# Attention in units of two key tiles by half of the queries, with projections for two heads at once through DRAM

## The reference

```python
lat = layer_norm(latents)                  # the 1024 tokens, after a norm without weights
q = lat @ Wq                               # 16 heads of 64
kv = concatenate([layer_norm(x), lat]) @ Wkv   # 6404 + 1024 = 7428 keys
dots = einsum('bhid,bhjd->bhij', q, k) * 64 ** -0.5
attn = softmax(dots)
out = einsum('bhij,bhjd->bhid', attn, v)   # 1024 queries x 64 per head
x = x + out @ Wout
```

## Time and profile before

| | us |
|---|---|
| median of 3 runs | 2882.32 (2880.21 to 2882.97) |
| span of the profiled execution | 2884.0 |
| PE busy | 2658.8 (92%) |
| DVE busy | 2348.5 (81%) |
| ACT busy | 2271.1 (79%) |
| POOL busy | 55.4 (2%) |

### The profile page before, as it was taken

The page is one execution under the profiler, slowest core; times in us unless marked ns, Lnnn a source line. Parts: engine busy times, 40 slices in busy tenths (PEclk is TensorE's granted clock), DMA queues, the critical chain, the costliest instruction groups (busy, mean ns, idle before and its releaser), DMA issues. The chain is left out here.

```text
span 2884.0 us, 93692 instructions
## 1 busy us (share of the span) xinstructions
PE 2658.8 (92%) x35639; PEld 1734.1 (60%) x35639; DVE 2348.5 (81%) x3328; ACT 2271.1 (79%) x2645; POOL 55.4 (2%) x95
## 2 busy tenths in 40 slices
PE   2799999999999999999999999999999999959996
PEld 1256665656565656565656566666656566747884
DVE  8789897979797979798888888888979797547864
ACT  4889897979797979797979798988979795426652
POOL 2100000000000000000000000000000000012001
PEclk9999999999999999999999999999999999979998
DMA  2000000000000000000000000000000000060000
GB/s 75 1 2 1 2 1 2 1 2 1 2 1 1 1 1 1 1 2 1 2 1 2 1 2 0 2 1 2 1 2 0 2 1 2 8 169 1 2 2 10
DMA packets 16345, 22.30 MB, mean 8 GB/s; under 512 B 1960, under 2 KB 13808, under 8 KB 15728
## 3 DMA queue, kind: packets, MB, share of 16 engines
q1 hardware_dynamic: 12816, 14.55, 1.7%
q10 hardware_dynamic: 3296, 4.10, 0.5%
HBM read 18.13 MB, written 0.52 MB: 6 GB/s over the span
## 5 line engine op out<-in xcount | busy, mean ns | idle before, releaser
L800 DVE TENSOR_TENSOR att_prob_low<-att_prob 128x1024 f16<-128x1024 f32 (+1 forms) x944 | 1153.7, 1223 | 196.7 <-ACT att_prob L678 195.9
L678 ACT ACTIVATE att_prob<-all_banks 128x1024 f32<-128x1024 f32 (+1 forms) x944 | 966.0, 1025 | 112.8 <-PE all_banks L565 32.6
L672 ACT ACTIVATE att_scores<-all_banks 128x1024 bf16<-128x1024 f32 x768 | 783.2, 1024 | 0.9 <-PE all_banks L495 0.6
L553 PEld LDWEIGHTS all_banks<-att_v,att_prob 128*128 128x128 bf16 x7552 | 538.3, 99 | 117.5 <-issue 16.1
L553 PE MATMUL all_banks<-att_v,att_prob 128*128 (+1 forms) x7552 | 597.7, 193 | 5.1 <-ACT att_prob L678 5.1
L554 PE MATMUL all_banks<-att_v,att_prob 128*128 (+1 forms) x7552 | 598.5, 195 | 0.0
L554 PEld LDWEIGHTS all_banks<-att_v,att_prob 128*128 128x128 bf16 x7552 | 506.0, 98 | 101.6
L535 PE MATMUL all_banks<-att_qc,att_kc 128*128 (+1 forms) x1888 | 562.5, 379 | 0.0
L535 PE MATMUL all_banks<-att_qd,att_kd 128*128 (+1 forms) x1888 | 562.0, 379 | 0.0
L495 PE MATMUL all_banks<-att_kc,att_qc 128*128 (+1 forms) x1792 | 534.3, 380 | 19.0 <-ACT att_scores L672 14.2
L774 DVE TENSOR_TENSOR att_running<-att_running,att_scores 128x1024 bf16<-128x1024 bf16 x768 | 525.9, 685 | 13.9 <-ACT att_scores L672 13.5
(11 more groups left out here) (276 smaller groups left out, 2810.3 us busy)
## 6 DMA issues: line engine op xcount, KB each, us to landing
prep_ctx<-in_ctx SPq DMA_DIRECT2D x5, 640.0 KB, 8.6
later_ctx<-in_ctx SPq DMA_DIRECT2D x1, 3200.0 KB
experts_up<-in_L_ffn_f SPq DMA_DIRECT2D x1, 2048.0 KB, 8.3
prep_wkv<-in_L_xattn_Wkv ACTq DMA_DIRECT2D x1, 1024.0 KB, 12.3
all_X<-in_x SPq DMA_DIRECT2D x1, 512.0 KB, 4.5
prep_wq<-in_L_xattn_Wq ACTq DMA_DIRECT2D x1, 512.0 KB, 14.5
wout_w<-in_L_xattn_Wout SPq DMA_DIRECT2D x1, 512.0 KB, 4.1
out<-all_X SPq DMA_DIRECT2D x2, 256.0 KB, 2.5
```

Source lines behind the costliest of these rows:

```text
L553: pe.matmul(O[:, j // 4, o:o + DH + 1], w, high, start=False, stop=False, skip_group_check=True)
L672: act.activation(o[:, :], banks[:, :, :].rearrange("p a q -> p (a q)"), ACT.Copy).then_inc(max_copied, 1)
L678: act.activation(prob[t % 2][0:n, :], S[t % 2][0:n, :], ACT.Exp, scale=SCALE).then_inc(exp_done, 1)
L800: dve.tensor_tensor(prob_low[t % 2][0:n, :], p, p.bitcast(BF16)[:, 1:2 * TOKENS:2], op=ALU.subtract)\
```

## The change

The attention is written anew. The stages around it stay, except that the weights `wk_h`, `wq_h` and their low parts are kept once instead of doubled (ACT makes three copies for five, POOL three subtractions for five).

- **Units.** The 1024 queries are taken in two halves. A unit is two key tiles by 512 queries; a head has 60: 29 pairs and the tile of 4 keys, for each half. `prob` and `prob_low` have three buffers each instead of two. `O` takes one bank instead of two.
- **Splits on two engines.** `by_pool`: POOL computes 44 of the 60 `prob_low` of a head, DVE those of units 1, 5, 9, ... and the last.
- **Maxima.** A slot is one product of 128 queries with at most 512 keys; there are 120 per head (8 tiles of queries by 15 chunks, the last chunk of 260). ACT does not copy them. DVE reduces from PSUM, both slots of a unit in one operation over banks 4 and 5 (`take_two`), or singly where one of the two is the short chunk. The slots of head b+1 begin at unit 24 of head b (`OFFSET`) and end at unit 23 of head b+1 itself; the second half of the maxima is needed there only at unit 30.
- **Projections.** Two heads at once: 17 tasks of K and Q during the even head of the pair before, 15 tasks of V during the odd one, one in every third unit (`side_task`), through bank 6. ACT copies the high part to a staging tile (`copy_task`), DVE subtracts (`split_task`), SP writes both to DRAM tensors, and loads them into `kc`, `kd`, `qc`, `qd`, `v` at the first unit of a head (`load_kq`, `load_v`) or at unit 51. ACT waits for the write from two tasks before.
- **Loop.** One loop of 7 rounds with two heads unrolled in each; heads 14 and 15 stand behind it. POOL has a loop of 16 rounds.

The core of the diff:

```diff
+            def max_slot(m, e, n, turn):
+                j, c = divmod(n, K_CHUNKS)
+                ...
+                pe.wait_ge(max_taken, 2 + m * SLOTS + n - 1)
+                pe.matmul(X[n % 2][:, 0:kwidth(c)], qc[:, e, j * P:(j + 1) * P],
+                          kc[:, e, c * BANK:c * BANK + kwidth(c)], start=True, stop=True).then_inc(max_scored, 1)
+            def head(b, e, with_max, projecting, i):          # PE
+                for g in range(UNITS):
+                    p = g % SIDE
+                    ...
+                    if p:
+                        apply_high(b, e, g, i)
+                    if slots:
+                        max_slot(m, me, n, i if m is b else i + e)
+                    if p >= 2:
+                        apply_low(b, e, g - 2)
+                    side_task(b, e, g, with_max, projecting, i)
+                    if slots:
+                        max_slot(m, me, n + 1, i if m is b else i + e)
+                    next_score(b, e, g, with_max)             # unit g + 2
+                    ...
+            def take_two(m, n):                               # DVE
+                if K_CHUNKS - 1 in (n % K_CHUNKS, (n + 1) % K_CHUNKS):
+                    take(m, n)
+                    take(m, n + 1)
+                else:
+                    dve.wait_ge(max_scored, m * SLOTS + n + 2)
+                    both = part[:, :, :].rearrange("p j c -> p (j c)")[:, n:n + 2]
+                    dve.tensor_reduce(both, pers.banks[:, 4:6, :], axis=AX.X, op=ALU.max).then_inc(max_taken, 2)
+                for g in range(UNITS):                        # DVE, one head
+                    ...
+                    if t is not None:
+                        split_task(i + 1, t)
+                    if not by_pool(g):
+                        split(b, g)
+                    if slots:
+                        take_two(m, n)
+                for g in range(UNITS):                        # POOL, one head
+                    if by_pool(g):
+                        pool.wait_ge(exp_done, EXP0 + b * UNITS + g + 1)
+                        pool.wait_ge(low_done, LOW0 + b * UNITS + g - 2)
+                        p = prob[g % NP][:, :]
+                        pool.tensor_tensor(prob_low[g % NL][:, :], p, p.bitcast(BF16)[:, 1:4 * BANK:2],
+                                           op=ALU.subtract).then_inc(split_pool, 1)
+            def copy_task(i, n):                              # ACT
+                if n < KQ_TASKS:
+                    r = n % NR
+                    act.wait_ge(kq_out[r], OUT0 + 32 * ((i - 1) * len(range(r, KQ_TASKS, NR)) + n // NR))
+                    copy_kq(i, n, Y, stage_h[r])
+            def load_kq(m):                                   # SP
+                e = m % 2
+                sp.dma_start(kc[0:DH, e, :], k_high[rows(m), :]).then_inc(k_in[e], 16)
+                sp.dma_start(kc[DH:P, e, :], k_high[rows(m), :]).then_inc(k_in[e], 16)
+                ...
+                sp.dma_start(kd[0:DH, e, :], k_low[rows(m), :]).then_inc(k_in[e], 16)
+            for n in range(KQ_TASKS, TASKS):                  # PE, ahead of head 0
+                pe.wait_ge(y_split, n - 3)
+                project(0, n, pers.banks[:, n % 4, :])
+                for x in FIRST_SLOTS[n - KQ_TASKS]:
+                    max_slot(0, 0, x, 0)
-            def between_heads(kind):
-            def copy_slot(m, j, half, c, slot, banks=X):
-            def take_slot(m, j, half, c, slot, fold=True):
-            def fold_tile(m, j, half):
```

More of the change, by code:

```diff
@@ L351, in stage_attention @@
+        zeros = sc.sb("zeros", [P, 4 * (DH + 1)], F16)
         warm = sc.sb("warm", [1, 1])
[L352 to L359 removed]
@@ new lines, in apply_low @@
+            def apply_low(b, e, g):
+                wait_split(pe, b, g)
+                for i, t in tiles(g):
+                    for q in range(4):
+                        w = prob_low[g % NL][:, i * BANK + q * P:i * BANK + (q + 1) * P]
+                        o = q * (DH + 1)
+                        last = pe.matmul(O[:, o:o + DH + 1], w, v[:, e, t, 0:DH + 1], start=False, stop=True,
+                                         skip_group_check=True)
+                last.then_inc(low_done, 1)
@@ new lines, in head @@
+            def head(b, e, with_max, projecting, i):
+                for g in range(UNITS):
+                    if g + 1 < UNITS:
+                        exp(b, g + 1)
+                    elif with_max:
+                        exp(b + 1, 0)
+                    n = task_at(e, g) if projecting else None
+                    if n is not None:
+                        copy_task(i + 1, n)
+                    elif g == BACK_AT:
+                        place_top(b, e, 1)
+                    elif g == FRONT_AT and with_max:
+                        place_top(b + 1, 1 - e, 0)
@@ new lines, in _ @@
+            act.wait_ge(constants, 1)
+            act.activation(warm[:, :], zeros[0:1, 0:1], ACT.Exp).then_inc(exp_done, EXP0)
+            for n in range(KQ_TASKS):
+                if n >= NF:
+                    act.wait_ge(first_out[n % NF], 32 * (n // NF))
+                copy_kq(0, n, pers.banks[:, n % 4, :], FIRST_H[n % NF])
+            act.wait_ge(filled, 3)
+            for n in range(KQ_TASKS, TASKS):
+                copy_v(0, n, pers.banks[:, n % 4, :])
+            place_top(0, 0, 0)
@@ new lines, in head @@
+            def head(b, e, with_max, projecting, i):
+                for g in range(UNITS):
+                    m, _, n = slots_at(b, e, g)
+                    slots = with_max or m is b
+                    t = task_at(e, g - 1) if projecting and g else None
+                    if t is not None:
[4 more added lines that the diff above has]
+                        take_two(m, n)
+                        if n + 2 in (SLOTS // 2, SLOTS):
+                            finish_max(m, 0 if n + 2 < SLOTS else 1)
+                    if g % SIDE == PAIRS:
+                        normalize_half(b, g // SIDE)
@@ new lines, in _ @@
+            for n in range(KQ_TASKS):
+                split_kq(0, n, pers.banks[:, n % 4, :], FIRST_H[n % NF], FIRST_L[n % NF])
+            for n in range(KQ_TASKS, TASKS):
+                split_v(0, n, pers.banks[:, n % 4, :])
+                for x in FIRST_SLOTS[n - KQ_TASKS]:
+                    take(0, x)
+                    if x + 1 == SLOTS // 2:
+                        finish_max(0, 0)
+            with dve.Fori(0, HEADS // 2 - 1) as it:
+                head(2 * it, 0, True, True, it)
+                head(2 * it + 1, 1, True, True, it)
```

798 lines of the change are left out of this document (357 added, 441 removed).

## The result

The changed kernel takes 2937.77 us (median of 4 runs, 2931.45 to 2938.16), the kernel before, run beside it, 2882.64: ratio 1.0188, 95% interval 1.0174 to 1.0203. The forecast was 2846. The profiled span is 2936.1 us, 52.1 more than before, and 88 more than the sum of the prediction.

The account below looks back on a forecast made before the run. PE was taken as the bound, with ACT and DVE right behind. Start 168, heads 2293 and later stages 387 summed to a span of 2848 us, so a run of 2846; 8 in 10 range 2740 to 2965.

Parts of the forecast that it names:

- the term for the loop jumps: At the loop over pairs of heads: 7 rounds x 3.7 = 26 us of PE waiting for instructions.
- held copy: In even heads, ACT's third copy waits for a write behind loads, delaying exponentials: about 5 us per pair at half rate.
- The third rival: At even heads' loads, DMAs hold ACT or lengthen instruction waits: 35 to 84 us, giving 2881 to 2930; chance 0.20.
- PE's own work: In each head with projections, PE's products, slots, projection tasks and spreading of maxima: 131.4 us per head.
- the spreading: Spreading of the maxima on PE: 8 products of 0.155 us, 1.2 us per head.
- The reduction: Joint DVE read of a unit's two slots takes 1.22 us; PE waits 0.17 us, 52 times: 8.8 us per head.
- DVE's full probability splits: Ahead of joint reductions on DVE: 5 meeting projection splits cost 3.8 us per head, 5 meeting none 0.3.
- POOL, its port: POOL's 44 splits per head, 2.12 us each, never run together with DVE's on the shared port; no cost counted.
- Start: Before the heads: first slots at 98 us, slots and V tasks 56 us, heads begin at 168, between 158 and 185.
- head 14: Head behind the loop, without projections: 121.0 + 8.8 + 1.3 = 131.1 us.
- head 15 with its end: Last head, with 48 of 120 slots: 105.9 + 4.3 = 110.2 us.
- The first rival: In the heads, PE never waits: 2093 us, span 2648; chance of half this gain or more 0.13.

Follow-up runs that it names:

- experiment 2: Changed kernel with every slot read by its own DVE reduction instead of a joint one per pair, order of products kept: 2741.47 us.
- Experiments 3: Changed kernel with the next head's K, Q and V loads issued at the eighth unit of an even head, behind the jump: 2933.82 us.
- Experiment 4: Changed kernel with the loop over seven pairs of heads written out on PE, ACT and DVE, so without a jump there: 2884.36 us.
- 7: Changed kernel with every slot read singly and the loop over pairs written out on PE, ACT and DVE: 2699.26 us.
- 8: Changed kernel with single reads, no jump, and DVE taking half a start round's slots before splitting its V task: 2699.84 us.
- 6: Changed kernel with loads at the eighth unit of an even head and three staging buffers instead of two: 2888.39 us.
- experiment 9: Changed kernel with single reads, the loop over pairs written out, and three staging buffers instead of two: 2654.23 us.
- experiment 5: Changed kernel with every full unit's probability split on POOL, leaving DVE only the two short ones: 2911.01 us.

## Why the prediction was wrong, step by step

The stated range, 2740 to 2965, holds the measured time, but the forecast was a faster kernel and the measured one is slower.

**The step that failed is the term for the loop jumps.** It read 7 x 3.7 = 26 us, the gap of the kernel before. The pair with single reads (279.1 us) and the one without jump or held copy (266.3) differ by 12.8 us, against 3.7 in the sum: 9.1 a pair, 64 us in all. In the kernel of experiment 2 PE's standstill is 9.2 us of the 12.8 ahead of the slot product and some 1.3 just behind it; the remaining 2.4 go with the lower clock behind the gap, an estimate by difference. The step took over a gap measured with no DMA in flight to a place where the same change had just put 5.2 MB of loads.

The third rival had the loads in the right place, named both ways in which they cost time (a held copy, a longer wait for instructions, 12 us per pair), gave 2881 to 2930, below the 2937.77 measured, and got a chance of only 0.20. Experiments 3, 4, 7 and 8 show the held copy taking over where the jump's long gap is gone; in 6 and 9 a third buffer ends it. In the changed kernel itself it was the jumps: its ACT waited for such a write only once, in head 0, where PE lost 3.5 us:

```profile
ACT att_stage_h L698 <- DMA q_low<-att_stage_l: 5.9, 1, 5.9
```

Does this one term turn the sign? Taken as above the sum would have been 2848 + 64 = 2912, above the 2884.0 of before, while all the other terms put right together give 2875. But the 12.8 us are those of the kernel with single reads. Experiment 4 takes the jumps alone out of the changed kernel and gains 53 us, 27 more than the 26 of the sum, which makes 2875 too; with the held copy that had come in the jumps' place there (some 10 us, an estimate from its six waits of 1.2 and the 6.4 for 3.5 in head 0) it is 2885. So this term is the largest error, and with PE's own work beside it the sum is clearly above 2884; whether it turns the sign by itself depends on which kernel's rows price it.

**PE's own work.** 131.4 us a head; the run in which PE never waits has 133.1. Of the 1.7 us, 0.9 are the spreading: the sum took the earlier trace rows's x16 for sixteen products, but an f32 product leaves two records, so a head's eight products cost 2 x 1.09 us and not 1.2. Another 0.3 is arithmetic: 112 slots of 0.22 and 8 of 0.11 are 25.5 us, not 25.2. Timeline of the kernel of experiment 9:

```profile
370.86 1.09 PE L576 MATMUL all_banks<-all_ident,att_top 128*64 128x128 f32 x8
```

Over 14 heads the term is 24 us short.

**The reduction: right in its mechanism.** 1.22 us taken, 1.224 measured; 1.75 from second slot to next slot, 1.77 measured; the wait with DVE's splits 13.3 us a head, 12.6 measured (304.3 less 279.1, halved). That the two agree so well is in part luck. A joint unit waits 0.21 us (2.24 less 2.03), not 0.17: 10.8 us a head (experiment 5's pair less experiment 2's, halved) where 8.8 was taken. DVE's full probability splits cost 1.8 (experiment 5) where 4.1 was charged. The reduction's wait and DVE's splits take 25 us of a pair, three quarters of the 34 us (300.4 before, 266.3 at best) that the change frees. The prediction charged this in full and still came out ahead by 5.9 us a head for want of the other two terms.

**POOL, its port: no cost, as forecast, but not for the reason given.** A split takes 1.99 us, 2.12 were taken, and all of them on POOL slow nothing (experiment 5). The prediction had POOL done with the port before DVE's split begins; in the trace 187 POOL splits meet one and are lengthened by it. It costs nothing because POOL, idle for 1074 us, has the time.

**Start.** 168 predicted, 180.9 measured. The first loads let the first slot go at 105.0, not 98: they were issued at 87.7, some 3 us later than the sum had them, and took 17 us, not 14. The rounds of V tasks take 5.6 us, not 56/12 = 4.7. Timeline of the changed kernel:

```profile
87.71 0.54 SPq L458 DMA_DIRECT2D att_kc<-k_high  x1
...
105.02 1.01 PE L568 MATMUL all_banks<-att_kc,att_qc 128*128 128x512 f16 x2 [20.73 <-issue]
...
119.59 0.76 DVE L782 TENSOR_TENSOR att_stage_v<-all_banks,att_stage_v 128x256 f16<-128x256 f32 x2 [1.23 <-ACT att_stage_v L706]
```

The path through DRAM costs a standstill of 20.7 us, and in each round DVE waits for PE's task and ACT's copy, 0.6 to 1.3 us, which the prediction took to lie beside its reductions. The "issue" of the second row is the wait for the loads, which the profile doesn't name there.

**The rest.** From first high product to first high product (at 180.87, 2307.38 and 2443.21 us in the changed kernel), heads 0 to 13 took 2126.5 us for 2052 with the jumps, head 14 took 4.7 more than forecast, head 15 with its end 0.4 less, the stages behind 3.9 less. Together with the start's 13 this is the 88 us measured. The terms above, 64 for the jumps and loads and 24 for PE, less 10 for reads and splits, give 78 of the 74.5 in heads 0 to 13; the last pair has no jump behind it, where the sum had one.

**The first rival** (PE unhindered, chance 0.13) gave 2093 us for the heads. The kernel of experiment 9 has 2088.2. That is near by luck: the 2093 hold 26 us for jumps that this kernel does not have, and PE's own work was taken 24 us too low. What stood between the changed kernel and this one was one reduction's form, one jump and one buffer.

## What to carry to other kernels

A wait of 0.2 us on the engine that bounds the kernel, repeated 800 times, outweighs what fewer operations save on an engine that idles (73 us of DVE here, for 196 us of the kernel): read two slots with two instructions if the first can run under other work. A measured gap holds for the traffic around it; where a change puts loads next to a loop's jump or writes behind loads in one queue, price the jump and the writes anew. And an edit that shows no gain may have moved the wait: look for where it went before dropping it.

## What the runs showed of the hardware that was not expected

- A jump that PE, ACT and DVE take together stops PE for 7.9 to 9.3 us with 5.2 MB of loads just issued and for 2.2 to 3.6 us without them, for the same body of two heads. The first instruction packet starts 3.8 to 4.3 us after PE stops in the one case and 1.2 to 1.5 us before it in the other. Straight code under the same loads (181 GB/s) loses almost nothing, 0.8 of 20 us. The loads themselves moved at 171 to 262 GB/s in the windows of the heads, about half of the 422 that the preparation reached, as the third rival supposed at its dearer end.
- Code written out for seven pairs is no slower per head than the loop: 146.5 us in odd heads against 155.4 less the jump's 8.3.
- A 128 KB write lands after 1.7 to 1.9 us in the median, and after some 17 us when 5.2 MB of loads stand in front of it in its queue: issued by 505.5, and the copy that waits for it starts at 523.0.
- A DVE reduction of 1024 elements over two banks takes 1.22 us, one of 512 takes 0.69, and two behind each other 1.29: joining saves 0.07 us of DVE's time and delays the first slot's release by 0.5.
- Where a POOL split and a DVE split overlap, the one that started second is the longer: POOL's up to 2.87 us for 1.89, DVE's (in head 15) up to 2.82 for 1.22.
